# A two-layer graph attention kernel: ten score blocks for eleven, x read transposed, and row maxima spread through DRAM

## The reference, cut to what matters

```python
h = jnp.maximum(_layernorm(x, axis=-1), 0.0)          # eps 1e-5
# two layers, the same code with other weights:
    u = jnp.einsum('bid,bjd->bij', h, h) / sqrt(384)   # symmetric: u[i,j] = u[j,i]
    a = jax.nn.softmax(u, axis=-1)
    delta = a * adjacency_matrix
    attn = delta / (jnp.sum(delta, axis=-1, keepdims=True) + 1e-10)
    hl = h @ wl.T + b_l;  hs = h @ ws.T + b_s;  hr = h @ wr.T + b_r
    ctx = (attn * upper) @ hl + diag(attn)[..., None] * hs + (attn * lower) @ hr
    h = relu((ctx - mean) / sqrt(var + 1e-12) * g + beta)
out = x + h
```

## Time and profile before

| | |
|---|---|
| median of three runs | 1216.45 us |
| the profiled execution's own time | 1216.47 us |
| its span (first to last instruction) | 1214.7 us |
| TensorE matmul busy | 1200.9 us, 99% |
| TensorE weight load busy (beside the matmuls) | 1178.6 us, 97% |
| VectorE busy | 917.0 us, 75% |
| GpSimd busy | 561.3 us, 46% |
| ScalarE busy | 515.0 us, 42% |
| moved | 60.85 MB, mean 50 GB/s |

### The profile page before, as it was taken

How to read it: one execution, slowest core, us unless ns; L and a number is a source line. 1 busy time by engine, 2 the same in 40 slices (tenths; PEclk the granted TensorE clock), 3 DMA queues, 4 the chain that set the end, 5 groups by cost and what they waited for, 6 DMA issues and landing times.

```text
span 1214.7 us, 18788 instructions
## 1 busy us (share of the span) xinstructions
PE 1200.9 (99%) x7146; PEld 1178.6 (97%) x7146; DVE 917.0 (75%) x2034; ACT 515.0 (42%) x1061; POOL 561.3 (46%) x624
## 2 busy tenths in 40 slices
PE   9999999999999999999999999999999999999997
PEld 7899999999999999999999999999999999999997
DVE  6567995679955898558985599865997659975688
ACT  4346433355333453334543444434344353434532
POOL 4465353554534545344543354442545424544346
PEclk9999999999999999999999999999999999999999
DMA  8001320012200131001310013100231002210000
GB/s 303 21 21 37 111 79 1 1 61 88 78 2 1 61 113 53 1 1 62 113 53 1 1 62 113 53 1 1 72 103 53 1 1 93 81 53 1 1 27 27
DMA packets 37002, 60.85 MB, mean 50 GB/s; under 512 B 2352, under 2 KB 27952, under 8 KB 36912
## 3 DMA queue, kind: packets, MB, share of 16 engines
q1 hardware_dynamic: 36624, 59.26, 14.8%
q10 hardware_dynamic: 288, 0.39, 0.1%
HBM read 47.06 MB, written 12.58 MB: 49 GB/s over the span
## 4 chain that ended last, share of the span: by engine, by line
PE 93%; DVE 4%; ACT 1%; DMA 1%; issue 1%; POOL 0%; SPq 0%; DVEq 0%
PE rot_ps L275 16%; PE rot_ps L276 16%; PE rot_ps L274 16%; PE u_ps L274 14%; PE u_ps L276 14%; PE u_ps L275 14%; PE rot_ps L340 3%; PE u_ps L332 1%; DMA x_norm<-x_dram 1%; PE rot_ps L349 1%; DVE et_lo L622 0%; DVE proj L650 0%; DVE x_stats L559 0%; DVE z L687 0%; ACT x_norm L419 0%
## 5 line engine op out<-in xcount | busy, mean ns | idle before, releaser
L881 POOL TENSOR_TENSOR hw_lo<-proj,hw_hi 128x384 fp32r<-128x384 f32 x256 | 280.8, 1112 | 323.6 <-ACT hw_hi L471 323.6
L274 PE MATMUL rot_ps<-w_hi,ht_hi 128*128 128x384 f32 x1152 | 389.6, 338 | 1.3 <-DVE proj L650 1.3
L275 PE MATMUL rot_ps<-w_lo,ht_hi 128*128 128x384 f32 x1152 | 385.7, 335 | 0.0
L276 PE MATMUL rot_ps<-w_hi,ht_lo 128*128 128x384 f32 x1152 | 385.5, 335 | 0.0
L274 PEld LDWEIGHTS rot_ps<-w_hi,ht_hi 128*128 128x128 f32 x1152 | 216.5, 188 | 1.6 <-DVE proj L650 1.6
L275 PEld LDWEIGHTS rot_ps<-w_lo,ht_hi 128*128 128x128 f32 x1152 | 216.5, 188 | 0.0
L276 PEld LDWEIGHTS rot_ps<-w_hi,ht_lo 128*128 128x128 f32 x1152 | 216.3, 188 | 0.0
L444 ACT ACTIVATE u_off<-u_ps 128x384 f32<-128x384 f32 x64 | 28.0, 438 | 363.9 <-PE u_ps L276 363.8
L650 DVE TENSOR_TENSOR proj<-rot_ps,bias 128x384 f32<-128x384 f32 x256 | 138.5, 551 | 51.7 <-PE rot_ps L276 51.7
L471 ACT ACTIVATE hw_hi<-proj 128x384 fp32r<-128x384 f32 x256 | 125.5, 518 | 86.5 <-DVE proj L650 85.9
L893 POOL TENSOR_TENSOR dg<-et_hi,tri 128x256 fp32r<-128x256 f32 x128 | 103.4, 808 | 126.7 <-PE u_ps L276 126.7
(11 more groups left out here) (89 smaller groups left out, 2047.6 us busy)
## 6 DMA issues: line engine op xcount, KB each, us to landing
out_dram<-z SPq DMA_DIRECT2D x64, 192.0 KB, 1.9
x_norm<-x_dram SPq DMA_DIRECT2D x15, 768.0 KB, 4.4
adj_a<-adj_t_dram SPq DMA_DIRECT2D x8, 1024.0 KB, 5.3
adj_b<-adj_t_dram SPq DMA_DIRECT2D x8, 1024.0 KB, 5.5
x_a<-x_dram SPq DMA_DIRECT2D x8, 768.0 KB, 4.6
x_b<-x_dram SPq DMA_DIRECT2D x8, 768.0 KB, 4.7
w_stage<-w_t_dram SPq DMA_DIRECT2D x4, 576.0 KB, 5.4
e_sb<-w_t_dram SPq DMA_DIRECT2D x1, 576.0 KB, 4.9
```

The source lines that it names most:

```text
L274: pe.matmul(dst, a_hi, b_hi, start=first and m == 0, stop=False)
L275: pe.matmul(dst[:, 0:b_lo.shape[1]], a_hi, b_lo, start=False, stop=False)
L276: done = pe.matmul(dst, a_lo, b_hi, start=False, stop=last and m == n - 1)
L881: pool.tensor_tensor(hw_lo[:, t, n, :], proj[:, t % 2, n, :], hw_hi[:, t, n, 0:dim].bitcast(F32), ALU.subtract).then_inc(hw_lo_done, 1)
```

## The change

1. Scores: tile 0 computes blocks 0 to 2, tile 1 blocks 1 to 3, tile 2 blocks 2 and 3, tile 3 blocks 0 and 3 (two separated blocks): ten in all. Six mirror transposes instead of five. They stand directly behind projection (0,0), in the order of tiles 1, 2, 3, 0, and ScalarE copies blocks of all four tiles first. The mirrors of tiles 3 and 0 wait for all four copies.
2. Features of x: the host hands over x transposed (`x_t`) as well. It is loaded into `xt_sb`. x in rows is loaded only for its statistics; means and reciprocal deviations are stored to DRAM and loaded back, spread over all partitions (512 KB). GpSimd subtracts the mean (three operations of 512 columns, in steps 0 and 2, behind the low halves of tile 1), VectorE scales with the rectifier (three operations), ScalarE rounds. There is no turn in steps 0 and 3. VectorE takes the statistics of both next graphs in step 1.
3. Row maxima: stored to DRAM (512 single values) and loaded back as a row on all partitions by two DMAs of SyncE, the second of which waits for the first. No transposes, no bank, no copy by ScalarE.
4. Attend(0) waits for each `et_lo` as it comes to it; `round_h` waits for all low halves of the projections, since its buffer is now `proj`.

```diff
-    U_FROM = [0, 1, 2, 2]
-    off_at = [0, 3 * P]
+    SCORED = [slice(0, 3), slice(1, 4), slice(2, 4), slice(0, 4, 3)]
+    OFF_BLOCKS = [slice(1, 3), slice(2, 4), slice(3, 4), slice(0, 1)]
+    OFF_AT = [0, 2, 4, 5]
+    MIRROR_ORDER = (1, 2, 3, 0)
+    MIRRORED = [[(3, 5)], [(0, 0)], [(0, 1), (1, 2)], [(1, 3), (2, 4)]]
...
+            def store_x_rows(graph):
+                sp.wait_ge(x_rstd_done, graph + 1)
+                sp.dma_start(rows_dram[graph % 2].rearrange("(q p t) -> p q t", q=2, t=TILES),
+                             x_mv[:, graph % 2, :, :]).then_inc(x_rows_stored[graph % 2], 16)
+
+            def spread_x_rows(graph):
+                sp.wait_ge(x_rows_stored[graph % 2], 16 * ((graph + 1) // 2))
+                sp.dma_start(flat(x_norm, 0, 2 * n_rows),
+                             rows_dram[graph % 2:graph % 2 + 1, :].to_broadcast([P, 2 * n_rows])).then_inc(x_rows_spread, 16)
...
             def pair(it, first, last):
+                next_a, next_b = it * 2 + 2, it * 2 + 3
+                if not last:
+                    sp.wait_ge(xt_scaled, KB * (next_a - 1))
+                    load_stat_rows(next_a)
+                    sp.wait_ge(ht_lo_done, LEAD_T + at(it, 0, KB, THREE))
+                    load_xt(next_a)
...
+                if not last:
+                    sp.wait_ge(x_stats_done, next_a * XS + TILES)
+                    load_stat_rows(next_b)
+                    store_x_rows(next_a)
+                    store_x_rows(next_b)
+                    spread_x_rows(next_a)
...
                 for g in range(2):
                     s = 2 + g
+                    sp.wait_ge(max_done, at(it, s, TILES, N_E))
+                    sp.dma_start(max_dram[g].rearrange("(t p) -> p t", p=P), neg_max[:, :],
+                                 allow_slow_non_contiguous=True).then_inc(max_stored, 16)
+                    sp.wait_ge(max_stored, 16 * (2 * it + (g + 1)))
+                    sp.dma_start(m_rows, max_dram[g:g + 1, :].to_broadcast([P, n_rows])).then_inc(max_spread, 16)
                     if not last:
                         sp.wait_ge(masked, at(it, s, TILES, FOUR))
                         sp.dma_start(adj_sb[g][:, :, :], rows(adj_t, it * 2 + (2 + g))).then_inc(adj_loaded[g], 16)
                         if g == 0:
+                            sp.wait_ge(xt_scaled, KB * next_a)
+                            spread_x_rows(next_b)
+                        else:
                             sp.wait_ge(ht_lo_done, LEAD_T + at(it, s, KB, THREE))
-                        else:
-                            sp.wait_ge(t_ready, LEAD_T + at(it, s, KB, THREE))
-                        sp.dma_start(x_norm[:, :, :], rows(x, it * 2 + (2 + g))).then_inc(x_norm_loaded, 16)
+                            load_xt(next_b)
...
                 project(0, 0)
+                for t in MIRROR_ORDER:
+                    mirror(t)
                 project(0, 1)
-                for t in range(1, TILES):
-                    mirror(t)
...
                 else:
-                    row_sum(0)
+                    for t in range(TILES):
+                        row_sum(t)
                     round_proj(0)
-                    row_sum(1)
-                    row_sum(2)
-                    row_sum(3)
-                    copy_max()
...
+                if s == 1 and not last:
+                    x_stats_of(next_a, range(TILES))
+                    x_variance(next_a)
                 if layer == 0:
+                    evacuate(0, 0)
                     mask(0)
-                    evacuate(0, 0)
                     evacuate(0, 1)
...
                     evacuate(1, 1)
+                    if s == 1 and not last:
+                        x_stats_of(next_b, range(0, 2))
                     e_low(1)
                     e_low(2)
                     evacuate(2, 0)
...
+                    if s == 1 and not last:
+                        x_stats_of(next_b, range(2, TILES))
                     e_low(3)
+                    if s == 1 and not last:
+                        x_variance(next_b)
                     diagonal(0)
                     evacuate(2, 1)
...
-                    row_max(0)
                     evacuate(0, 0)
+                    for t in range(TILES):
+                        row_max(t)
                     evacuate(0, 1)
-                    for t in range(1, TILES):
-                        row_max(t)
...
+                if s == 0:
+                    for db in range(KB):
+                        x_scale(next_a - 1, db)
...
+                    if s in (0, 3) and i < 2:
+                        for db in ((0,), (1, 2))[i]:
+                            h_low(db)
+                    if s == 2 and not last and i in (1, 2):
+                        for db in ((0, 1), (2,))[i - 1]:
+                            x_scale(next_a, db)
...
+            def x_centre(graph):
+                pool.wait_ge(xt_loaded, 16 * graph)
+                pool.wait_ge(x_rows_spread, 16 * graph)
+                for db in range(KB):
+                    pool.tensor_tensor(xt_sb[:, db, :], xt_sb[:, db, :], mean_b, ALU.subtract).then_inc(xt_centred, 1)
...
                 proj_low(0)
                 set_ones()
                 proj_low(1)
+                if s == 0:
+                    x_centre(it * 2 + 1)
+                if s == 2 and not last:
+                    x_centre(it * 2 + 2)
```

More of the change, by code:

```diff
@@ L198, in all_pairs, with blocks, stat_rows @@
                 body(it, it == 0, it == pairs - 1)
+        def blocks(columns, which):
+            return columns.rearrange("p (b c) -> p b c", c=P)[:, which, :]
         def rows(dram, graph):
             return dram[graph].rearrange("(t p) n -> p t n", p=P)
+        def stat_rows(dram, graph):
+            return dram[graph].rearrange("(p t) n -> p t n", t=TILES)
         def flat(tile, lo, hi):
@@ L497, in round_h @@
                     act.activation(ht_hi[:, parity, db, :], ht_f32[:, db, :], ACT.Copy).then_inc(ht_hi_done, 1)
-                for t in range(2):
+                for t in range(TILES):
                     copy_off(t)
@@ L513, in step @@
                     round_e(3)
-                    if s == 0 and not first:
-                        x_normalise(it * 2 + 2, range(0, 2))
-                else:
-                    row_sum(0)
+                else:
+                    for t in range(TILES):
+                        row_sum(t)
                     round_proj(0)
-                    row_sum(1)
-                    row_sum(2)
-                    row_sum(3)
-                    copy_max()
                     exp(0)
@@ L529, in step @@
                     round_e(1)
-                    if s == STEPS - 1 and not last:
-                        x_normalise(it * 2 + 3, range(0, 2))
                 if first and s == 1:
@@ L537, in step @@
                     round_e(3)
-                if s == 0 and not first:
-                    x_normalise(it * 2 + 2, range(2, TILES))
-                elif s == STEPS - 1 and not last:
-                    x_normalise(it * 2 + 3, range(2, TILES))
                 round_proj(3)
-                if first and s == 0:
-                    x_normalise(2, range(TILES))
                 if not final:
                     for db in range(KB):
-                        round_h(db)
+                        round_h(db) if s in (1, 2) else round_x(db)
                 if first and s == 0:
@@ L780, in step @@
                         diagonal(t)
[L781 to L784 removed]
+                if s in (1, 2):
                     for db in range(KB):
                         h_low(db)
+                if s == 0:
+                    for db in range(KB):
+                        x_scale(next_a - 1, db)
                 if final:
@@ L832, in step @@
                 add_x(TILES - 1)
-                if ahead is not None:
-                    x_shift_of(ahead)
             all_pairs(lambda it, first, last: [step(it, s, first, last) for s in range(STEPS)])
@@ L902, in step @@
                     pool.wait_ge(den_done, at(it, s, 0, ONE))
+                if first and s == 0:
+                    x_rstd_of(1)
+                if s == 1 and not last:
+                    x_rstd_of(it * 2 + 2)
                 proj_low(0)
@@ L908, in step @@
                     proj_low(2)
-                    if first and s == 0:
-                        x_rstd_of(2)
                     triangles(1)
+                    if s == 1 and not last:
+                        x_rstd_of(it * 2 + 3)
                     proj_low(3)
@@ L946, in step @@
                 rstd_of(slice(0, TILES), 1)
-                if s >= 2 and not last:
-                    x_rstd_of(it * 2 + (s + 1))
             all_pairs(lambda it, first, last: [step(it, s, first, last) for s in range(STEPS)])
```

250 lines of the change are left out of this document (116 added, 134 removed).

## The result

| | median us | range | |
|---|---|---|---|
| before | 1216.6 | 1216.28 to 1217.08 | |
| after | 1377.3 | 1374.46 to 1378.98 | ratio 1.132, 95% interval 1.130 to 1.133 |

The forecast was 1244 us, its range 1204 to 1274. The kernel became slower, as forecast, but by 161 us in place of 28, far outside the range.

The account below looks back on a forecast made before the run. TensorE, busy 99%, was taken as the bound. Seven pairs at +3.9 us (-5.1 saved, stalls 1.5, 1.9, 3.3, 2.3) and a last at +0.2 add 27.5 to 1216.5: 1244 us, 8-in-10 range 1204 to 1274.

Parts of the forecast that it names:

- The store: SyncE's store of 512 separate 4-byte row maxima to DRAM in steps 2 and 3: taken as 2.3 us.
- S: Time from a step's first score matmul to the first shift by the maxima: 15.4 us; 16.1 in step 3.
- The load: Load of the maxima row into 128 partitions (256 KB), behind the store: 2.6 us, ends 1.8 and 4.4.
- Step 2: Graph a's second layer: attend(0) waits for GpSimd's triangles, ready at S + 15.5, wanted at 27.6; stall 3.3 us.
- step 3: Graph b's second layer: attend(0) waits for VectorE's low half, ready at S + 11.9, wanted at 25.7; stall 2.3 us.
- Rival 3: Much slower: 4-byte pieces cost like the 5.6 us row, S grows by 3.3, kernel 1297 us; chance 0.08.
- TensorE's savings: Whole kernel: scores 15.7, maxima 7.0, turn 19.8, mirrors -3.2; sum 39.3 us, 5.1 in a usual pair.
- Step 0: Graph a's first layer: attend(0) waits for GpSimd's low half, delayed by three subtractions; stall 1.5 us, ends 0.5 and 2.5.
- Step 1: Graph b's first layer: projection number 10 waits for VectorE's evacuation behind statistics; stall 1.9 us, ends 1.2 and 2.5.
- The first pair "as usual": First pair counted at the usual +3.9 us; x's statistics 0 to 3 us late, against a turn wait that goes.
- A clock under 1.00 after the stalls: TensorE's granted clock dropping after stalls would add time that the forecast had not counted; no size given.
- rival 1: Faster: short round trip, 1.0 us store and 1.8 us load, 3.5 us of stall a pair, kernel 1203; chance 0.22.

Follow-up runs that it names:

- e9: Changed kernel with the maxima stored as 512 4-byte pieces 64 bytes apart, and the load taking a row of x instead: 1268.1 us, 1.042.
- e5: Kernel before plus extra stores and loads by SyncE in an idle place of step 1, read by no computing engine: time of before (1216.7 and 1216.8 with its sister run).
- e10: e2 with the moves of e7 and e8, and VectorE's three scalings moved from the end of step 2 into step 3: 1181.95 us, 0.9718.
- e8: e2 with GpSimd's three subtractions moved later, behind the low halves and triangles that TensorE waits for: 1200.3 us, 0.987.
- e7: e2 with graph b's statistics of x in step 1 moved behind VectorE's evacuations: 1210.8 us, 0.995.
- e2: Changed kernel with its third part alone undone, the maxima spread by four transposes on TensorE and a ScalarE copy: 1220.1 us, 1.003.
- e12: e10 with the maxima's round trip through DRAM put back, stored as 128 pieces of 16 bytes: 1252.9 us, 1.030.

## Why the prediction was wrong

Its sign and its chain were right; the round trip's time was mis-sized, the store above all.

- **The step that failed: "The store ... I take 2.3" and with it "S = 10.2 + 2.3 + 2.6 + 0.3 = 15.4, ends 13.3 and 20.5".** The store measured 8.0 (7.4 to 10.2), the load behind it 4.5 (3.0 to 4.8), S 23.7 and 23.3: 8.3 and 7.2 late. I took nearly the value of the 192 KB row (1.9) since its queue was quiet like this one; the row of 4-byte pieces (5.6) I put down to the crowd at the start. e9 and e5 show that the choice was wrong by its kind: it is how the pieces lie, for with a quiet queue adjacent ones take 8.5. Even my upper end for it (that load's 5.6) was too low. The load, 2.6 carried down from larger ones, takes 3.4 even where nothing is in its way (e9, e5). Lateness of 8.3 and 7.2 us in eight pairs is 124 us; with the forecast's 28 and the 5.5 of the first step it makes 157 of the 161.
- **The formulas behind S hold.** Step 2 without a stall is 36.65 (e10's 37.1 less the 0.44 of transposes), step 3 35.3. With the measured S, step 2 is 36.65 + (23.74 + 15.5 - 27.6) = 48.3 (measured 48.15), step 3 is 35.3 + (23.32 + 11.9 - 25.7) = 44.8 (measured 45.37). With e9's 16.1 the first gives 40.7 (measured 40.6 in that pair, 40.0 to 40.7 in pairs 0 to 6). Where TensorE waits is not where the forecast put it: most of the time goes at a bank that VectorE has not evacuated (6.9 us in that step 2), and only 1.3 at the attention. The end of the step is the same, for the chain behind S sets it.
- **Rival 3** named the mechanism, with the place right (steps 2 and 3 pay whole) and 80 us too little; it had 0.08.
- **TensorE's savings**: priced steps without stalls, 35.3 and 36.6, and, with the transposes kept, 37.1 and 35.8. e10: 35.4, 36.55, 37.1, 35.9. The forecast's sum with the transposes kept is 1216.5 - 39.3 + 7.0 = 1184.2. e10 took 1181.95; its first step is 4.3 us shorter than before where 1.7 were priced, and with those 2.6 us taken off, the sum is within 0.4 us of it.
- **Step 0**: stall 1.5 forecast, 1.6 measured (36.91 - 35.3), gone in e8. The cause is the one named, the way only in part, and that the size fits is in part luck: of TensorE's idle time in that step 0.30 us are on GpSimd's low half and 0.83 on a bank that VectorE evacuates late. Beside the subtractions VectorE's own instructions are longer, as the same low half shows, first in the kernel after, then in e8:

```profile
711.85 1.31 DVE L666 TENSOR_TENSOR et_lo<-e_sb,et_hi 128x512 fp32r<-128x512 f32 x1
```

```profile
619.58 0.75 DVE L679 TENSOR_TENSOR et_lo<-e_sb,et_hi 128x512 fp32r<-128x512 f32 x1
```

- **Step 1**: 1.9 forecast, 1.4 measured (37.93 - 36.55), gone in e7. The wait is at the place named, 1.1 us at 21.3 into the step. In **step 2** the subtractions' share could be read only with S small: e2 38.0, e8 37.09, 0.9 us.
- **The first pair "as usual"**: its first step grew by 5.3 us where a usual one was priced at -0.2, wrong by 5.5. The rows of x's statistics were stored amid the first loads, GpSimd's subtractions waited for them and the low halves stood behind (TensorE waited 4.9 and 2.0 us there, on L926). e8, which takes them out of the low halves' way, has the first step at 36.0.
- **A clock under 1.00 after the stalls** was named as uncounted. It came, and by the waits it was hidden: see below.
- **Slips in its working**, small beside the rest: step 0's terms give 27.1 - 25.7 = 1.4, not 1.5; step 1's give 23.7 - 21.6 = 2.1, not 1.9; rival 1 takes 0.8 and 1.3 for the low ends of steps 0 and 1, which stand as 0.5 and 1.2.

The Trainium skill's page "DMA: Bandwidth & Descriptors" (Anatomy of one DMA) gives about 2.0 us fixed plus bytes / 436e3, measured on GpSimd's path. That is an estimate of 2.0 for the store and 2.6 for the load. The traces agree for pieces 64 bytes apart or 128 pieces of 16 bytes (probes and medians 1.8 to 2.4), not for adjacent 4-byte ones (8.0), and the load took 3.4 to 4.5. The Trainium skill says on the same page (Specifications) that below 512 bytes there is a read-modify-write; that spoke against the change, and I gave it no weight of its own. It alone does not tell the stores apart: 512 x 64 B are below 512 bytes too, and took 1.8.

## What to carry to other kernels

Price a small store to DRAM by how many separate pieces fall side by side, not by its kilobytes: in the probes here up to two in 64 bytes landed in 1.5 to 2.3 us, four in 1.8 to 2.9, eight in 4.2 to 5.1, sixteen in 8.5 to 10.2 (32 such pieces alone in 3.3). A two-transfer round trip costs about 5 us here even at its best (1.44 + 3.77 in one step of e12), against 0.44 us of transposes on the engine that was the bound. It stands before the longest chain of the step, and there the transposes' way is the shorter one too: in e2 the shift starts 3.2 and 2.3 us behind the last row maximum (VectorE's evacuations included). So price such a move by how much later the next step of the chain starts, not by the work that it takes from the bound engine. Of the forms that bring the maxima back, the 16-byte pieces were the cheapest tried, and e12 lost 71 us by them against e10; a spaced store with a spaced load back was not tried. When work is moved to engines with free time, put it behind what the bound engine waits for: nearly the same instructions, in another order, turned 1220 us into 1182.

## What the runs showed of the hardware

**The load behind the slow store is slow too.** In e5, 256 KB spread over the partitions took 5.1 us directly behind the adjacent store, 3.8 behind the 16-byte one, 3.4 for x's values behind the spaced one, 3.1 from 128 separate rows, one run each. In the kernels the medians are 4.5 behind the adjacent store, 3.7 behind the 16-byte one and 3.4 for x's values. Whether the store's tail or the source's address does it isn't separated.

**TensorE at half clock, at no cost that the waits show.** The matmuls behind the long wait of that step 2 of the kernel after (start, length, operation, idle before):

```profile
795.62 0.69 PE L344 MATMUL rot_ps<-w_hi,ht_hi 128*128 128x384 f32 x1 [6.93 <-DVE proj L694]
...
800.90 0.52 PE L345 MATMUL rot_ps<-w_lo,ht_hi 128*128 128x384 f32 x1
801.22 0.39 PE L346 MATMUL rot_ps<-w_hi,ht_lo 128*128 128x384 f32 x1
801.45 0.33 PE L344 MATMUL rot_ps<-w_hi,ht_hi 128*128 128x384 f32 x1
801.62 0.33 PE L345 MATMUL rot_ps<-w_lo,ht_hi 128*128 128x384 f32 x1
```

After 6.93 us without a matmul, 18 of them start 0.32 us apart (the first two 0.48), at a granted clock of 0.50, the 1.2 GHz level, and from 801.45 on 0.17 apart, at 2.4 GHz. That is some 2.6 us more. But TensorE still waits 0.65 us for GpSimd's low half and 0.62 for its triangles at the end of the chain, S + 15.3, and VectorE works without a gap from the shift on, GpSimd from its subtractions on, so the step would be as long without the loss. Step 3 of that pair has the same: half clock behind 6.5 us without a matmul, and 0.35 us of waiting for VectorE's low half at the attention. A stall can thus hold its own clock loss, and by these waits the granted clock of 0.89 explains none of the two steps' length; no run kept the clock up. Before, the clock of every step was 1.00.
